# Query tiles loaded one step further ahead, expert chunks moved out of the last three attention steps, and the work around the end of attention put in another order

## The reference

```
mod = silu(c) @ wmod                                # six rows of 512 per batch: sa, ca, ga, sb, cb, gb
h   = layernorm(x) * (1 + ca) + sa
x   = x + ga * attention(h)                         # 16 heads of 128, causal, softmax, output projection
h   = layernorm(x) * (1 + cb) + sb
x   = x + gb * (shared_swiglu(h) + top2_of_8_experts(h))   # experts of width 352, shared width 704
```

## Time and profile before

| | us |
|---|---|
| median of 3 runs | 1685.36 (1681.59 to 1687.44) |
| the profiled execution, its own time | 1688.79 |
| its span in the trace | 1687.0 |
| mean granted clock of PE, as a share of full speed | 0.965 |

### The profile page before, as it was taken

How to read it: one execution, slowest core, us unless ns; L and a number is a source line. 1 busy time by engine, 2 the same in 40 slices (tenths; PEclk the granted TensorE clock), 3 DMA queues, 4 the chain that set the end, 5 groups by cost and what they waited for, 6 DMA issues and landing times.

```text
span 1687.0 us, 29744 instructions
## 1 busy us (share of the span) xinstructions
PE 1561.8 (93%) x8844; PEld 1382.3 (82%) x8845; DVE 1032.9 (61%) x2255; ACT 727.0 (43%) x1728; POOL 663.5 (39%) x713
## 2 busy tenths in 40 slices
PE   6899999988989999999999999778998899999997
PEld 3677778877988888889899888677898788888886
DVE  5866666756766767767767667577657322222257
ACT  3532223346655656556656556442231233232232
POOL 2113333544465544555555556675221211111043
PEclk9999999997999999999999999889999899999999
DMA  7336545576546465655556564678213354655555
GB/s 247 131 137 208 203 177 193 212 255 215 175 137 196 136 197 167 196 148 174 165 176 177 167 200 131 187 232 320 87 38 132 150 181 180 252 202 193 180 170 180
DMA packets 203199, 303.82 MB, mean 180 GB/s; under 512 B 80304, under 2 KB 142128, under 8 KB 195968
## 3 DMA queue, kind: packets, MB, share of 16 engines
q1 hardware_dynamic: 193136, 276.56, 49.0%
q0 software_dynamic: 5680, 18.62, 3.8%
q10 hardware_dynamic: 4320, 7.87, 1.5%
HBM read 187.35 MB, written 115.64 MB: 180 GB/s over the span
## 4 chain that ended last, share of the span: by engine, by line
PE 38%; DMA 25%; issue 10%; POOL 10%; SPq 8%; DVE 7%; ACT 1%; POOLq 1%; another core or an unknown queue 0%; DVEq 0%; ACTq 0%
PE bank L1378 19%; PE bank L1473 15%; DMA q_raw<-q_transposed 13%; DMA slot_results<-y_sb 5%; DMA ch_raw<-wexp 4%; POOL ch_lo L876 3%; POOL q_hi L874 3%; SPq L747 2%; SPq L746 2%; POOL ch_hi L874 2%; SPq L749 2%; PE bank L1391 1%; PE bank L1632 1%; PE bank L1658 1%; SPq L678 1%
## 5 line engine op out<-in xcount | busy, mean ns | idle before, releaser
L1378 PE MATMUL bank<-w,xt_hi 128*128 (+2 forms) x1136 | 286.7, 334 | 9.6 <-issue 4.3
L1378 PEld LDWEIGHTS bank<-w,xt_hi 128*128 128x128 f32 x1136 | 198.5, 191 | 22.1 <-issue 11.6
L874 POOL CAST q_hi<-q_raw 128x512 fp32r<-128x512 f32 x64 | 70.7, 1105 | 299.6 <-DMA q_raw<-q_transposed 299.6
L1378 PE MATMUL bank<-w,xt_lo 128*128 (+2 forms) x568 | 185.6, 327 | 0.0
L1215 ACT ACTIVATE prob<-prob,row_inv 128x128 f32<-128x128 f32 (+3 forms) x256 | 137.1, 560 | 101.0 <-DVE row_inv L2026 101.0
L1378 PE MATMUL bank<-wv_hi,h_hi 128*128 128x256 f32 x512 | 153.8, 300 | 22.4 <-POOL wv_lo L876 18.3
L2151 DVE TENSOR_TENSOR ht_lo<-bank,ht_hi 128x128 fp32r<-128x128 f32 (+1 forms) x213 | 48.4, 283 | 194.8 <-ACT ht_hi L1312 191.1
L1378 PE MATMUL bank<-w,ht_hi 128*128 (+3 forms) x426 | 143.4, 418 | 17.7 <-DVE ht_lo L2151 17.6
L1203 ACT ACTIVATE prob<-bank,neg_max 128x128 f32<-128x128 f32 (+3 forms) x256 | 133.9, 526 | 44.3 <-DVE neg_max L2018 43.9
L1378 PE MATMUL bank<-wv_lo,h_hi 128*128 128x256 f32 x512 | 149.9, 293 | 0.0
L1378 PE MATMUL bank<-wv_hi,h_lo 128*128 128x256 f32 x512 | 149.8, 293 | 0.0
(11 more groups left out here) (227 smaller groups left out, 4136.7 us busy)
## 6 DMA issues: line engine op xcount, KB each, us to landing
keys<-k_ring SPq DMA_DIRECT2D x64, 512.0 KB, 3.0
ch_raw<-wexp SPq DMA_DIRECT2D x128, 170.0 KB, 2.8
experts_hi<-ch_hi SPq DMA_DIRECT2D x128, 170.0 KB, 2.0
experts_lo<-ch_lo SPq DMA_DIRECT2D x128, 170.0 KB, 2.3
w<-experts_hi SPq DMA_DIRECT2D x10, 2176.0 KB, 8.7
w<-experts_lo SPq DMA_DIRECT2D x10, 2176.0 KB, 15.3
q_transposed<-q_out SPq DMA_DIRECT2D x64, 256.0 KB, 2.0
k_even<-keys SPq DMA_DIRECT2D x16, 1024.0 KB, 6.1
```

The lines of the kernel that those rows point to most:

```text
L874: pool.tensor_copy(hi, raw).then_inc(split_hi, 1)
L1378: ins = pe.matmul(dst, a, m, start=(k == 0), stop=(k == last))
```

## The change

- **Queries.** SP loads the queries of step n+2 in step n, after `split_q(1)` has freed the buffer and after the first two chunks of the step. Before, it loaded those of step n+1 in step n, after the keys.
- **Chunks.** `chunks_of` gives each step its chunks: 2 in step 0, then 4, 5, 5, 4 at b = 0 to 3 of a pair, none in the last three steps. At b = 0 no chunk is loaded for the next step; b = 1 loads its first two itself. The total stays 128. On POOL, two chunks stand between `split_q(0)` and `split_q(1)`, the others behind `split_q(1)` and, at b = 3, behind the `wv` split.
- **Step 0.** `values(2)` and `values(3)` move behind `scores(1)` and `scores(2)`. On ACT and DVE `v_part(1)` moves to where the other steps have it.
- **End of stage 1.** The load of `h` parts (`load_h(0)`) moves from half 25 to half 26, behind the key stores of that half; a dummy exponential on ACT moves earlier.
- **Norm of batch 0.** In step 30 the statistics stand behind the transposed parts and behind `maxima(0)` of the next step instead of between the maxima; one row tile is made in step 30 (before: two), three in step 31 in other places (before: two). The rows are stored as tile 0, tile 1, tiles 2 and 3 (before: in one store), each `xin` tile loaded when its store has landed.
- **Norm of batch 1.** Its statistics move from step 31 to behind the last output tiles, and its rows from between them to behind job 0.
- **Last projection.** `turn_rows(0)` moves from behind the last `weigh(1)` to before the last `weigh(0)`. The gate product of job 0 moves ahead of the last four output tiles, which get four banks of their own; the up product follows them.
- **SP in step 31.** `mods`, `xr`, then the row stores and `xin` loads, then the shared weights.

```diff
+def chunks_of(p, b, first):
+    if first:
+        return 0, 2
+    if isinstance(p, int) and p == HP - 1 and b:
+        return 0, 0
+    return (-2, 2, 7, 12)[b], (4, 5, 5, 4)[b]
...
 SP, stage 1
                     load_q(0, 0)
+                if v == NV - 2:
                     load_h(0)
...
 SP, step
-                if not last:
-                    if not first:
-                        sp.wait_ge(s_full, n * 6)
-                        load_k(n + 1, (b + 1) % 2)
-                    sp.wait_ge(q_ok, n * 2 + 2)
-                    load_q(p if b < B - 1 else p + 1, (b + 1) % B)
+                if not first and not last:
+                    sp.wait_ge(s_full, n * 6)
+                    load_k(n + 1, (b + 1) % 2)
+                if first:
+                    sp.wait_ge(q_ok, 2)
+                    load_q(0, 1)
+                if b == 1 and count:
+                    for q in range(2):
+                        sp.wait_ge(ch_ok, p * 18 + (at + q - 1))
+                        load_chunk(q)
+                if tail >= 0:
+                    load_mods(tail)
+                    load_xr(tail)
...
+                for q in range(min(count, 2)):
+                    chunk(q)
+                if not last and tail != 1:
+                    sp.wait_ge(q_ok, n * 2 + 4)
+                    load_q(p if b < B - 2 else p + 1, (b + 2) % B)
+                for q in range(2, count):
+                    chunk(q)
+                if last:
+                    sp.wait_ge(v_full, (NIT - 1) * 2)
+                    for k in range(2):
+                        store_h2(0, k, k + 1)
+                        sp.wait_ge(h2_st, 16 * (k + 1))
+                        sp.dma_start(xin[:, k, :].unsqueeze(1), rows_t[:, k:k + 1, :]).then_inc(xin_ld[k], 16)
+                    sp.wait_ge(v_full, NIT * 2)
+                    for k in range(2):
+                        sp.wait_ge(ch_st[k], 16 * NCH)
+                    load_shared(0, WG, WU)
+                    load_shared(1, WU, WD)
+                    load_shared(2, WD, WE)
+                    store_h2(0, 2, TT)
+                    sp.wait_ge(h2_st, 16 * 3)
+                    sp.wait_ge(xt_full, 1)
+                    sp.dma_start(xin[:, 0, :].unsqueeze(1), rows_t[:, 2:3, :]).then_inc(xin_ld[0], 16)
...
 PE, step
                 if first:
-                    for t in range(TT):
-                        values(t)
+                    values(0)
+                    values(1)
                     pe.wait_ge(half_ok, sum_count(NV - 1, C21))
                     scores(0, n, 0)
                     scores(1, n, 0)
+                    values(2)
...
                 scores(2, n, here)
+                if first:
+                    values(3)
...
+                else:
+                    turn_rows(0, 0, loaded(0, 0, False))
                 weigh(0)
...
 PE, behind the steps
-            pe.wait_ge(s_exp, NIT * 6)
-            turn_rows(0, 0, loaded(0, 0, False))
-            out_tile(NIT - 1, HP - 1, 0, (v_ok, 2 * NIT - 1))
...
             pe.wait_ge(we_ld[0], 32)
-            job(0, 0, 0, 0, route=True, prev=False, up_ld=(we_ld[1], 32))
+            half(0, 0, 0, 0, True)
+            for i in range(TT):
+                out_tile(NIT - 1, HP - 1, i, None)
+            pe.wait_ge(we_ld[1], 32)
+            half(0, 0, 0, 1, True)
+            turn_rows(1, 1, loaded(1, 1, False))
+            pe.wait_ge(wo_add, NIT * TT)
...
 DVE, step
-                if norm:
-                    c_stats(b - 2, 0)
...
-                if norm3:
-                    c_rows(0, 2)
-                    c_rows(0, 3)
-                if norm:
-                    c_stats(b - 2, 2)
-                    c_stats(b - 2, 3)
-                    c_moments(b - 2)
                 pt_part(0, 0)
                 pt_part(0, 1)
                 invert(5, n)
                 pt_part(0, 2)
+                if norm2:
+                    c_stats(0, 0)
+                    c_stats(0, 1)
+                if norm3:
+                    c_rows(0, 1)
+                v_part(1)
...
 DVE, behind the steps
-            c_rstd(1)
-            add_out(NIT - 1, B - 1, 0)
-            xt_part(0, 0)
-            for i in range(1, TT):
+            for i in range(TT):
                 add_out(NIT - 1, B - 1, i)
-                c_rows(1, i - 1)
-            c_rows(1, TT - 1)
+            for t in range(TT):
+                c_stats(1, t)
+            c_moments(1)
...
+                    if n == 0:
+                        c_rstd(1)
+                        for t in range(TT):
+                            c_rows(1, t)
```

More of the change, by code:

```diff
@@ new lines, in chunk @@
+                def chunk(q):
+                    s, to = (at + q) % 2, bass.ds((p * 18 + (at + q)) * CH, CH)
+                    sp.wait_ge(ch_ok, p * 18 + (at + q + 1))
+                    sp.dma_start(wx_hi_d[:, to], ch_hi[:, s, :].bitcast(F32)).then_inc(ch_st[s], 16)
+                    sp.dma_start(wx_lo_d[:, to], ch_lo[:, s, :].bitcast(F32)).then_inc(ch_st[s], 16)
+                    if not first and (b or q < count - 2):
+                        load_chunk(q + 2)
+                for q in range(min(count, 2)):
+                    chunk(q)
@@ L788, in _ @@
             sp.wait_ge(wo_add, NIT * TT)
-            for k in range(2):
-                sp.wait_ge(ch_st[k], 16 * NCH)
             load_w(E + 1, 1)
@@ L953, in step @@
                         waits.append((wo_full, n * TT))
[L954 to L971 removed]
+                    split(wo_raw[:, :, :], wo_hi[:, :, :], wo_lo[:, :, :], waits, wo_ok)
+                for q in range(min(count, 2)):
+                    chunk(q)
+                if not last:
+                    split_q(1)
+                if b == 3 and not at_end:
+                    split(wv_raw[:, :, :], wv_hi[:, :, :], wv_lo[:, :, :],
+                          [(wv_ld, p * 16 + 32), (v_full, n * 2 + 2)], wv_ok)
+                if tail == 1:
+                    c_seed_of(0)
+                for q in range(2, count):
+                    chunk(q)
+                if tail >= 0:
+                    c_pre(tail)
                 if last:
                     c_seed_of(1)
[L974 to L976 removed]
             walk_steps(pool, step)
@@ L1262, in step @@
                     bias_rows(2)
-                else:
-                    v_part(1)
                 for g in range(3):
                     pt_part(1, g)
+                if last:
+                    xt_part(0, 0)
                 o_part(0)
@@ L1340, in quad0 @@
                     job(n, i % 2, None if first and i == 0 else "shared", True,
[L1341 removed]
+                        n + 3, b + 1 if i == 1 else 0 if first and i == 0 else None, True)
             quad0(0, True)
```

152 lines of the change are left out of this document (59 added, 93 removed).

## The result

The changed kernel takes 1618.55 us (median of 4 runs, 1614.78 to 1621.66) against 1685.24 us for the kernel before beside it: a ratio of 0.9605, 95% interval 0.9574 to 0.9636. The forecast was 1622, with a range of 1607 to 1647. Two later comparisons on other chips gave 0.9666 [0.9641, 0.9692] and 0.9646 [0.9619, 0.9673]; the experiments on the same two chips are read against these. In the first of them the kernel before also had one slow run of 3041 us, which the ratio leaves out.

A forecast was written before the change was run, and what follows sets the result against it. A loop of POOL, SP and the query load, longer than PE's step, was taken to hold PE back. Start 3.5, 29 steps 50.7, step 30 12.8, step 31 -3.4: 63.6 us off 1685.4 gives 1622, range 1607 to 1647.

The forecast's parts named there:

- Queries: Middle 29 steps: queries a step ahead and chunks regrouped remove the listed waits; 50.7 us gained after allowances.
- POOL's new hours: Softmax chain of the 29 steps: DVE waits out POOL's running instruction; 0.1 us a step, 3 us in all.
- rival A: Softmax chain: DVE's wait for POOL is the rule, 0.5 us in 29 steps; 1633, up to 1645; chance 0.12.
- Step 30: Weigh(0) of step 29 to end of step 30: 8 us statistic stall goes, 25.9 us, a gain of 12.8.
- Step 31: Step 31 to the first down product: gets longer, 57.0 us against 53.65, a loss of 3.4.
- `xin` wait: Step 31: row tile 0's store stands behind the xr load, so PE idles about 6 us.
- eight row operations: DVE rows before ht_part(0), after step 31 begins: 0.75 to 1.6 us each, so 6 to 13 us.
- Start: Before values(0) of step 0: h loads go behind the key store; 3.5 us gained, ends 0 and 8.
- B: Middle: a new loop through SP's chunks keeps the wv split waiting, half the middle gain lost; 1647; chance 0.09.
- C: Middle: SP's in-order issues stall behind the query load, keys come late; 13 us stall gives 1694; chance 0.05.
- D: Middle: PE gives the idle time back as lower clock, steps of 22.5 us; 1662; chance 0.05.
- E: End, step 31 to first down product: goes well with short xin wait, gain up to 12; 1607; chance 0.07.

The follow-up runs named there:

- experiment 1: Kernel before, with only the queries of step n+2 loaded after the second chunk of step n; 1628.14 us, ratio 0.9721.
- experiment 2: Changed kernel, with the query load put back to one step ahead, ahead of the chunks; 1693.65 us, ratio 1.0114 to the kernel before.
- second repeat: Changed kernel run again untouched, on the third chip of the experiments; 1619.35 us, ratio 0.9646 to the kernel before.
- experiment 9: Changed kernel, with row tile 0's store and read-back ahead of the xr load, shared weights ahead of row tile 1's, in step 31; 1623.57 us.
- experiment 11: Changed kernel, with only the statistics of batch 2 moved behind the second shared job; 1616.99 us, ratio 0.9636 to the kernel before.
- experiment 10: Changed kernel, with the load of h for the next batch back in its old place, one half earlier; 1625.63 us.
- experiments 3 and 4: Changed kernel; 3: negated maximum one row at a time, 1624.79 us; 4: POOL waits for each residual operation's end before the next, 1621.28 us.

## Why the prediction was right

The mechanism and the sum hold; the sizes of single terms are off by up to 4 us and partly cancel. Three are off by 3.5, 3.3 and 3.8 us; that the sum is off by 4.0 only, since one of them has the other sign, is luck. As a ratio the forecast is 1622 / 1685.4 = 0.962, between the 0.9605, 0.9646 and 0.9666 measured.

*Queries.* Right, and shown from both sides: experiment 1 has the gain with nothing else, experiment 2 loses all of it (and 15 us more) with everything else in place. The loop of POOL, SP and the load was the bound of the middle. The term is 3.5 us too small: I had left 2 us for the wv split and 3 us for DVE's waits, and both came to nothing, while 3.0 us stayed, 2.2 of them in step 1 at its lower clock, for which I had left 1.5. The wv split's spare time of 2.6 us was enough.

*POOL's new hours.* The trace agrees with the rule quoted: in the clean step above POOL casts from 853.05 to 853.52, and DVE's instruction ends at 853.54.

```profile
853.05 0.47 POOL L900 CAST ch_hi<-ch_raw 128x340 fp32r<-128x340 f32 x1
...
842.86 0.17 DVE L2048 TENSOR_SCALAR neg_max<-row_max 128x2 f32<-128x2 f32 x1
...
853.26 0.28 DVE L2048 TENSOR_SCALAR neg_max<-row_max 128x2 f32<-128x2 f32 x1
```

It costs 0.11 us of the 0.4 that the chain can bear. In the middle POOL's runs are short and the early neg_max (842.86) finds POOL idle. Others there last up to 0.68 us, but PE is busy throughout, so rival A has nothing to live on. But "only that instruction's remainder" is too small as a bound: 5.11 and 3.64 us were measured in unbroken runs. The Trainium skill ("SBUF — State Buffer", section "SBUF: two separate sides", the bullets under its diagram) has the lock held for one instruction; these two rows show that DVE can also miss the boundary.

*Step 30.* 9.5 instead of 12.8: the missing 3.3 us are that stall of 3.6. Where it was absent the term was as forecast: in the second repeat values(0) of step 31 starts 25.5 us (1011.68 to 1037.18) behind weigh(0) of step 29, against 25.9. The cause named was the smaller one. I had put the late residual down to two chunks that wait for loads behind `mods` and `xr`. Experiment 1 keeps that wait (6.26 us), and step 30 still falls from 34.31 to 26.66 us, since POOL, which had stood 10.48 us for the queries just before, no longer does and reaches the residual 7.9 us sooner; with the chunks away it is 21.1.

*Step 31.* I had it longer by 3.4 us; it was shorter by 0.4. The `xin` wait came as forecast, 4.94 us against 6, and by the cause named (experiment 9). Too dear were the shared weights, which PE did not wait for at all (its gate product at 1069.61, 30.7 us behind the start of the step instead of 32, follows the weigh products), and the eight row operations: 0.75 us each with POOL idle, 6 us, the lower end of the 6 to 13 that the earlier trace rows seemed to allow. The last wait, DVE late with `ht_lo`, is confirmed by experiment 11.

*Start.* 2.9 against 3.5, but the load of `h`, named as the cause, is worth 0.8 us of it (experiment 10), and profiles of one kernel differ by 2.6 there.

*The rivals.* B falls with the 615.48 us. C: PE is busy throughout the 29 steps, so no issue of SP came late enough to count. D: behind step 1 the clock stays at 1.00 for 592 us; idle time removed is not given back. E came true in a small part, 4 us. C's number does not follow from its own terms: a stall of 13 us is 3.0 above the 10.0 (6.3 + 3.7) that fit, 87 us in 29 steps, which gives 1709 and not 1694; the range does not use it.

## What to carry to other kernels

When a helper engine waits long for a transfer, follow the loop of issue, transfer and split, and compare its length with the bound engine's step: moving one issue a step ahead took 55 us here, while the same chunks regrouped without it came out 15 us slower in the middle. After such a change, read the last pass anew, for the in-order queue that issues the transfers decides what is late there: some 9 us more lay in the order of a few DMAs and four statistics. Take a stall seen in one profile as a fact of this kernel only when a second profile of it has it.

## What the runs showed of the hardware

- A DVE instruction of 128x2 (0.17 us alone) beside an unbroken run of POOL operations lasted 1.32 to 1.34 us six times, 3.64 once and 5.11 once. The two long ones ended at POOL's first pause, the others with the running operation. With pauses of 0.1 us between POOL's operations it lasted 0.41 to 0.46 (three times), each time to the end of the running operation. Split into two of 128x1, it took 0.21 us for both while a POOL operation ran on (once).
- One kernel differs between executions more than small edits move it: the stretch behind the first down product took 527.2, 530.3 and 533.1 us in the three profiles of the changed kernel, which are on three chips. On one chip, experiments 3 and 4 took 534.3 and 529.8 us there, at the same instructions.
- On one chip the kernel before ran from 1669 to 1682 us in nine runs and the changed one from 1619 to 1625 in four. That a loop with a transfer in it scatters more is only argued.
